# Half-precision value chunks and evenly spread sums in an attention and convolution block

## The chip, the cores and the metric

The kernel runs on one core of one Trainium2 chip. The metric is the time of one execution on the device in microseconds (us).

## What is computed

The reference takes four images of 96 channels and 128 x 128 points, in f32, and adds two branches one after the other:

```
x = x + attention(groupnorm(x))
x = x + convolutions(groupnorm(x))
```

The attention normalizes over the channels, projects to 96 query and 48 key and value channels (24 and 24), and runs a depthwise 3 x 3 convolution over all 144:

```
q  = dwconv3x3(conv1x1(xn, q_w), q_dw)
kv = dwconv3x3(conv1x1(xn, kv_w), kv_dw)
k, v = split(kv)
attn = softmax(l2norm(q) @ l2norm(k).T * temperature)
out  = conv1x1(attn @ v, proj_w)
```

The contraction of `attn` runs over all 16384 points of an image, so it is a small matrix per head. The second branch is a 1 x 1, a 3 x 3, a 5 x 5 and a dilated 3 x 3 convolution, joined by a 1 x 1. Both group norms need sums over a whole image.

## The kernel before, in words

One program goes through the four images (`for b in range(B)`). In each, all engines follow the same order of stages: normalizing and projecting (L844 on PE), the depthwise convolution, the gram product of queries and keys (L902), softmax and attention (L937), and the joined convolutions in units of rows (L1012, L1017). Semaphores written out by hand set the order; each engine has its own list, and what stands behind a wait on an engine waits too. Names in capitals are constants of the program.

**The depthwise stage.** The 144 channels are cut into `DK` = 24 chunks of six: chunks 0 to 19 are queries and keys, 20 to 23 are values. In the planes of a chunk the points' rows lie on the partitions, so that a vertical tap is a product with a band matrix. For each chunk

- DVE builds the band matrices by masking the taps `V` (`bands`, L1493), into one of two buffers: the bands of chunk n start when chunk n-2 is through;
- PE multiplies (`depthwise`): an f32 chunk has three matmuls a channel (L869, which the trace shows as two records each), a chunk in the list `SPLIT` has nine f16 matmuls a channel (L874), on the high and the low half of planes and taps. Results go to three pairs of PSUM banks in turn;
- ScalarE copies the result out (`evict`): L1132 for queries and keys, which are kept as a high half, and L1129 for values, which go back to `Q` in f32;
- DVE forms the low half of queries and keys (`low_parts`, L1521).

GpSimd (POOL) cuts the planes of the chunks in `SPLIT` into halves beforehand, three steps a chunk (`split_chunks`, L692 to L694). Image 0 has no split chunk: there POOL prepares the weights of the convolutions instead. Once, in image 0 behind the strips, DVE cuts the taps into halves (`packed_taps`, L1506 to L1512), one run of chunks after the other. Chunks 6 to 17 of an image are a hardware loop on PE, the others are straight code.

**The sums of the next image.** Group norm needs the sums and the sums of squares of the next image before it starts. SP brings that image in 32 pieces (`AT`) of four rows through three buffers (`stage_rows`), a piece's load when the piece three before it is summed. Between its evictions ScalarE sums each piece twice with an accumulating activation (`next_sums`: L1140 plain, L1146 squared). Behind an even chunk stands one piece, behind an odd chunk two, until there are none left.

**Behind the stage.** DVE waits for all 32 pieces (`s_ns`), copies the first strip of queries and keys (`strip`, L1540), and adds up the sums (`moments`, L1395 to L1398). PE waits for the same sums and for the third step of the moments, makes the group mean's product (`group_mean`, L818), and goes on to the eight gram products (`gram`, L902):

```
pe.wait_ge(s_ns, (b + 1) * AT + START)
pe.wait_ge(s_qd, (b + 1) * DK - 1 + START)
group_mean(st, MEANX, sv + N_MEANN, 3)
```

**Setup.** Before image 0 DVE takes the statistics of that image (L1340) and the scales of the taps (L1361 to L1376, L1438 to L1440).

Of the kernel before, what the change touches and what calls it, by code (L numbers as in the profile page):

```python
# [25 lines left out]
def build_program(nc, x, ln_w, ln_b, q_w, q_dw, kv_w, kv_dw, proj_w, temperature, w1, w3, w5, wd, wf, out):  # L26
    f32, f16, bf16, i32 = mybir.dt.float32, mybir.dt.float16, mybir.dt.bfloat16, mybir.dt.int32
    ALU = mybir.AluOpType
    ACT = mybir.ActivationFunctionType
    AX = mybir.AxisListType  # L30

    B, C, H, W = x.shape
    P = 128
# [3 lines left out]
    KC = KV // 2  # L37
    HD = C // HEADS
    CO = C + KV
    QK = C + KC  # L40
# [4 lines left out]
    AT = H // AR  # L45
# [50 lines left out]
    with ctx:  # L96
# [38 lines left out]
        V = sb("V", [P, 3, 3 * CO])  # L135
# [10 lines left out]
        ps = ctx.enter_context(nc.psum_tensor("ps", [P, 8, BANK], f32))  # L146
# [21 lines left out]
        T = work[:, 1536:1536 + 2 * DM * BW].rearrange("p (i m x) -> p i m x", i=2, m=DM)  # L168


        SPLIT = (2, 4, 5, 7, 8, 10, 11, 13, 14, 16, 17, 19)
        SPLIT_RUNS = (slice(2, 18, 3), slice(4, 20, 3))
        NS = len(SPLIT)
        MASK = 6
        LOW, HIGH = 0, 1
# [66 lines left out]
        rawdw = Qf[:, 7392:7392 + 9 * CO].rearrange("p (m d) -> p m d", d=3)  # L242
# [15 lines left out]
        tapsum = Qf[:, 10200:10200 + QK]  # L258

        def col(i, n=C):  # L260
            return small[0:n, i:i + 1]
# [3 lines left out]
        OSC_MHALF, OSC_MSIXTH, OSC_SIXTH, OSC_THIRD, OSC_THIRDS, OSC_HALF = range(37, 43)  # L265
        QKS, CLAMP, WMAX, TMAX, BMAX = 43, 44, 45, 46, 47
        QSC, QINV = 26, 30
        MEANX, VARX, SAX, SBIX, MG2 = 23, 24, 27, 28, 29
        OSCS = ((OSC, 1.0), (OSC_MHALF, -0.5), (OSC_MSIXTH, -1.0 / 6), (OSC_SIXTH, 1.0 / 6), (OSC_THIRD, 1.0 / 3),
                (OSC_THIRDS, 2.0 / 3), (OSC_HALF, 0.5))  # L270
# [34 lines left out]
        s_vscaled = plain_sem("depthwise_taps_scaled")  # L305
# [5 lines left out]
        s_qd = sem("stored_chunk")  # L311
# [45 lines left out]
        s_wt = plain_sem("weights_placed")  # L357

        NLOADS = 13
        N_BOUND, N_RES, N_QKS, N_AMAX, N_WSC = 6, 9, 23, 28, 31  # L360
        N_QKV = N_WSC + len(OSCS) + 3
        N_COPIES = 4
        N_TURNED = 3 * (3 + 2)
        N_SPLIT = 13 + NRT * 6 + 2
# [182 lines left out]
        def _(pool):  # L547
# [115 lines left out]
            for b in range(B):  # L663
# [15 lines left out]
                def split_chunks():  # L679

                    pool.wait_ge(s_pq, (b + 1) * AT + START)
                    pool.wait_ge(s_out, b * UNITS * 16 + START)
                    pool.wait_ge(s_packed, 3 * len(SPLIT_RUNS))
                    steps = Steps(s_qs, (b - 1) * 3 * NS + START)

                    def step(ins):
                        steps.done(ins)
                        pool.wait_ge(s_qs, steps.value())
                    for m in SPLIT:
                        words = Q[:, m * DC:(m + 1) * DC, :].rearrange("p c h -> p (c h)")  # L690
# [76 lines left out]
        def _(pe):  # L767
# [63 lines left out]
            for b in range(B):  # L831
# [46 lines left out]
                for n in range(6):  # L878
                    depthwise(n, n, SPLIT.index(n) if n in SPLIT and b else None)
                with pe.Fori(0, 2) as k6:  # L880
                    for at in range(6):
                        depthwise(k6 * 6 + 6 + at, at, k6 * 4 + SPLIT.index(6 + at) if at % 3 and b else None)
                for n in range(18, DK):
                    depthwise(n, n, SPLIT.index(n) if n in SPLIT and b else None)

# [144 lines left out]
        def _(act):  # L1030
# [47 lines left out]
            for b in range(B):  # L1078
# [36 lines left out]
                if b < 1:  # L1115
                    act.wait_ge(s_V, N_TURNED)
                    act.wait_ge(s_dv, N_QKV)
                    act.activation(V[:, :, 0:3 * QK], V[:, :, 0:3 * QK], ACT.Copy, scale=col(QKS, P)).then_inc(s_vscaled, 1)
                    act.activation(V[:, :, 3 * QK:], V[:, :, 3 * QK:], ACT.Copy, scale=col(QINV, P)).then_inc(s_vscaled, 1)
                    act.wait_ge(s_dv, N_WSC)  # L1120
                    for k in range(5):
                        act.activation(folded[:, k], folded[:, k], ACT.Copy, scale=col(WSC)).then_inc(s_fold, 1)

                def evict(n):
                    k2, i = divmod(n, 2)
                    bank = 2 * (n % 3)
                    act.wait_ge(s_dw, b * DK + n + 1 + START)
                    if n >= 2 * GROUPS_QK:
                        act.activation(Q[:, n * DC:(n + 1) * DC, :].rearrange("p (k c) h -> p k (c h)", k=2),  # L1129
                                       ps[:, bank:bank + 2, 0:3 * H], ACT.Copy).then_inc(s_qd, 1)  # L1130
                        return
                    act.activation(HL[:, k2, :, DC * i:DC * (i + 1)].rearrange("p h (k c) -> p h k c", k=2),  # L1132
                                   ps[:, bank:bank + 2, 0:3 * H].rearrange("p k (c h) -> p h k c", c=3),
                                   ACT.Copy).then_inc(s_qd, 1)

                def next_sums(c, j, loads, first=False):

                    act.wait_ge(s_nl[j], loads * 16 + START)
                    act.wait_ge(s_ns, b * AT + c + START)
                    act.activation(stage[j], stage[j], ACT.Copy,  # L1140
                                   accum_out=nsums[:, bass.ds(c, 1)]).then_inc(s_nt, 1)
                    act.wait_ge(s_nt, b * AT + c + 1 + START)
                    if first:
                        act.activation(col(NSH), nsums[:, 0:1], ACT.Copy, scale=-1.0 / BANK).then_inc(s_nsh, 1)
                        act.wait_ge(s_nsh, b + 1 + START)
                    act.activation(stage[j], stage[j], ACT.Square, bias=col(NSH),  # L1146
                                   accum_out=nsums[:, bass.ds(AT + c, 1)]).then_inc(s_ns, 1)

                for n in range(DK):
                    k2, i = divmod(n, 2)  # L1150
                    evict(n)
                    for j in ((0,) if i == 0 else (1, 2)):
                        c = k2 * 3 + j
                        if c < AT:
                            next_sums(c, j, b * (11 if j < 2 else 10) + k2 + 1, c == 0)
                act.wait_ge(s_qd, (b + 1) * DK + START)

                def values(k):
# [168 lines left out]
        def _(dve):  # L1327
            v = nc.vector
            setup = Steps(s_dv)

            def link(steps, ins):
                steps.done(ins)
                dve.wait_ge(steps.s, steps.value())
# [18 lines left out]
            for k in range(3):  # L1352
# [9 lines left out]
                                        apply_absolute_value=True))  # L1362
# [11 lines left out]
            link(setup, v.tensor_scalar(col(BMAX, P).bitcast(i32), col(BMAX, P).bitcast(i32), 0x7F800000, None, ALU.bitwise_and))  # L1374
            link(setup, v.reciprocal(col(QKS, P), col(BMAX, P)))
            link(setup, v.tensor_scalar(col(QKS, P), col(QKS, P), 16384.0, None, ALU.mult))  # L1376
            assert setup.n == N_QKS
            statistics(6, len(TAKEN))

# [58 lines left out]
            link(setup, v.tensor_tensor(col(CLAMP, P), col(QKS, P), col(QKS, P), ALU.mult))  # L1438
            link(setup, v.tensor_scalar(col(CLAMP, P), col(CLAMP, P), 1e-24, None, ALU.mult))
            link(setup, v.tensor_tensor(col(QKS, P), col(QKS, P), col(QINV, P), ALU.mult))  # L1440
            assert setup.n == N_QKV

            for b in range(B):
# [36 lines left out]
                def bands(n, parts):  # L1480
# [5 lines left out]
                    dve.wait_ge(s_vscaled, 2)  # L1486
                    if b and n in SPLIT:
                        dve.wait_ge(s_packed, 3 * len(SPLIT_RUNS))
# [108 lines left out]
                with dve.Fori(0, SETS // 2) as k2:  # L1597
                    for k in range(2):
                        for j in range(2):
                            n = (b * (SETS // 2) + k2) * 4 + k * 2 + j  # L1600
# [263 lines left out]
                for r in range(OR):  # L1864
                    n = len(range(r, LASTR, OR))
# [30 lines left out]
```

## Time and profile before

| | |
|---|---|
| Time, median of 3 runs | 1664.78 us (1664.50 to 1666.73) |
| The profiled execution | 1664.77 us, of which the span from the first to the last instruction is 1663.0 us |
| Busy on PE, DVE, ScalarE, POOL | 97%, 88%, 63%, 39% of the span |
| Mean granted clock of TensorE | 0.975 of full speed |

The span is that of the profile's first to last instruction; the rest of the execution's time lies around it. A matmul's end is modelled, so a busy PE is not a PE at its peak. Times in the rows are microseconds from the span's start. The depthwise stages begin near 102, 510, 911 and 1312 us.

### The profile page before, as it was taken

The page shows a single profiled execution, that of the slowest core. Times are in us where ns is not written, and L with a number is a line of the kernel's source. Part 1 is how long each engine was busy: PE and PEld are TensorE (multiplying, and loading weights), DVE is VectorE, ACT ScalarE, POOL GpSimd, SP SyncE. Part 2 cuts the span into 40 slices and gives each one's busy share as a digit, 9 for nine tenths or more (in the row PEclk, how much of TensorE's full clock was granted, in tenths as well). Part 3 has the DMA queues.
Part 4 walks back from the last instruction along what each step waited for, and adds up shares of the span by engine and source line. Part 5 has one row for each costly group of instructions (what it writes and reads, how often), then busy time and mean ns, then how long its engine had stood idle before and what let it go on. Part 6 is the DMA issues. An engine that isn't in the chain of part 4 may idle for free.

```text
span 1663.0 us, 38439 instructions
## 1 busy us (share of the span) xinstructions
PE 1605.5 (97%) x13933; PEld 1524.3 (92%) x13933; DVE 1456.9 (88%) x1949; ACT 1040.2 (63%) x1667; POOL 655.7 (39%) x507
## 2 busy tenths in 40 slices
PE   6999989999999999999999999899999999899998
PEld 5999959999999986999999996899999999599998
DVE  6788789999789959999978986999988897799996
ACT  4877676555286868645546776765446677765651
POOL 4888031222289303232248903023226950312232
PEclk9999979999999997999999998899999999799999
DMA  7012205666502202666630220366661131054553
GB/s 197 0 42 73 71 5 138 171 164 180 151 18 59 81 16 48 158 169 178 171 101 15 73 67 1 89 175 176 170 167 48 34 85 36 16 137 127 145 149 100
DMA packets 105042, 166.37 MB, mean 100 GB/s; under 512 B 40266, under 2 KB 78763, under 8 KB 104780
## 3 DMA queue, kind: packets, MB, share of 16 engines
q1 hardware_dynamic: 81772, 138.95, 33.1%
q10 hardware_dynamic: 23168, 26.04, 5.1%
q8 instruction: 65, 1.06, 0.3%
q14 instruction: 37, 0.30, 0.1%
HBM read 52.20 MB, written 25.17 MB: 47 GB/s over the span
## 4 chain that ended last, share of the span: by engine, by line
PE 80%; DVE 9%; issue 6%; ACT 3%; SPq 1%; DMA 1%; DVEq 0%; ACTq 0%
PE ps L1017 41%; PE ps L869 14%; PE ps L844 12%; PE ps L874 7%; PE ps L902 3%; DVE region L1765 1%; PE ps L1012 1%; DVE region L1493 1%; ACT region L1237 1%; DVE region L1340 1%; ACT region L1168 1%; DVE region L1790 1%; ACT region L1193 1%; DVE region L1762 1%; ACT region L1218 0%
## 5 line engine op out<-in xcount | busy, mean ns | idle before, releaser
L1017 PE MATMUL ps<-region,W 128*96 128x256 f16 (+2 forms) x7140 | 790.6, 271 | 16.0 <-DVE region L1790 8.0
L1017 PEld LDWEIGHTS ps<-region,W 128*96 128x96 f16 (+1 forms) x7140 | 779.1, 122 | 19.8 <-DVE region L1790 9.5
L1493 DVE TENSOR_TENSOR region<-V,ps 128x2322 int32<-128x2322 int32 (+2 forms) x104 | 246.9, 2384 | 37.0 <-issue 30.9
L1237 ACT ACTIVATE region<-region 96x1584 f16<-96x1584 f32 (+2 forms) x80 | 98.4, 1272 | 287.5 <-DVE region L1699 287.5
L748 POOL TENSOR_TENSOR region<-region 96x528 f32<-96x528 f32 (+1 forms) x72 | 96.4, 1343 | 437.9 <-DVE region L1765 238.5
L869 PE MATMUL ps<-region 128*128 (+2 forms) x2160 | 248.7, 276 | 8.6 <-DVE region L1493 4.7
L869 PEld LDWEIGHTS ps<-region 128*128 128x128 f32 x2160 | 243.7, 192 | 12.4 <-issue 7.5
L844 PE MATMUL ps<-proj,region 96*128 96x240 f32 x1024 | 208.5, 367 | 0.0
L844 PEld LDWEIGHTS ps<-proj,region 96*128 96x128 f32 x1024 | 194.6, 190 | 12.8
L667 POOL TENSOR_TENSOR region<-region,cbias 128x576 f32 (+1 forms) x124 | 175.7, 1417 | 57.9 <-DVE region L1465 54.2
L738 POOL TENSOR_TENSOR region<-region,X 96x1536 f32<-96x1536 f32 x40 | 116.0, 2901 | 190.1 <-DVE region L1820 190.1
L1765 DVE TENSOR_TENSOR region<-region 96x1056 f16<-96x1056 f32 (+6 forms) x160 | 175.7, 1154 | 0.6 <-ACT region L1242 0.5
L1790 DVE SCALAR_TENSOR_TENSOR region<-ps,small,region 96x768 f32<-96x768 f32 (+1 forms) x176 | 163.9, 989 | 13.2 <-PE ps L1017 11.5
L714 POOL TENSOR_TENSOR region<-X 96x512 f32<-96x512 f32 (+1 forms) x16 | 29.1, 1841 | 268.5 <-PE ps L937 268.5
L874 PE MATMUL ps<-region 128*128 (+2 forms) x1944 | 120.2, 220 | 0.1
L874 PEld LDWEIGHTS ps<-region 128*128 128x128 f16 x1944 | 116.2, 98 | 2.6 <-issue 0.2
L1132 ACT ACTIVATE region<-ps 128x768 f16<-128x768 f32 x80 | 65.6, 820 | 81.1 <-PE ps L869 69.5
L1231 ACT ACTIVATE region<-region 96x1584 f16<-96x1584 f16 (+3 forms) x88 | 113.9, 1295 | 0.4
L1820 DVE TENSOR_TENSOR region<-region 96x256 f32<-96x256 f32 (+3 forms) x176 | 89.0, 546 | 24.2 <-DMA out_dram<-region 22.6
L1465 DVE TENSOR_TENSOR region<-ps,region 128x576 f32<-128x576 f32 x124 | 94.0, 758 | 12.3
L1086 ACT ACTIVATE region<-X,small 96x512 f32 (+1 forms) x128 | 101.6, 803 | 0.3 <-DVE small L1391 0.3
L1092 ACT ACTIVATE region<-ps 128x384 f32<-128x384 f32 x128 | 62.7, 490 | 54.0 <-PE ps L844 50.9
(249 smaller groups left out, 2139.8 us busy)
## 6 DMA issues: line engine op xcount, KB each, us to landing
region<-region SPq DMA_DIRECT2D x104, 247.5 KB, 4.2
region<-in_x_dram SPq DMA_DIRECT2D x128, 192.0 KB, 2.4
out_dram<-region SPq DMA_DIRECT2D x40, 576.0 KB, 4.3
region<-region ACTq DMA_DIRECT2D x72, 247.5 KB, 2.5
X<-in_x_dram SPq DMA_DIRECT2D x30, 576.0 KB, 6.2
region<-region SPq DMA_DIRECT2D x32, 247.4 KB, 5.1
X<-in_x_dram SPq DMA_DIRECT2D x19, 384.0 KB, 10.4
region<-region SPq DMA_DIRECT2D x24, 185.6 KB, 3.9
```

The lines of the kernel that those rows point to most:

```text
L667: pool.tensor_tensor(Q[:, :, bass.ds(t * AR, AR)].rearrange("p c r -> p r c"), pq[:, i], cbias[:].unsqueeze(1).broadcast_to([P, AR, CO]), ...
L738: pool.tensor_tensor(ob[:, 0:r * W], ob[:, 0:r * W], X[:, bass.ds(u * UR * W, r * W)], ALU.add).then_inc(s_res, 1)
L844: last = mm(ps[:, 2 * i + r // 2, r % 2 * 256:r % 2 * 256 + NP], y1[:, i, r * W:(r + 1) * W], proj[:], start=True, stop=True)
L869: last = mm(o[:, to], T[:, i, 3 * c + d, 0:W], src[:, of], start=k == 0, stop=k == 2)
L874: last = mm(o[:, to], T16[:, i, 3 * c + d, 0:W, te], parts[qe][:, of], start=k == t == 0, stop=k == t == 2)
L1017: last = mm(o, w, src, start=opens and k == 0, stop=k == len(steps) - 1, skip_group_check=g in (2, 4) or split and ck > 0)
L1086: act.activation(y1[:, i, :], X[:, bass.ds(t * BANK, BANK)], ACT.Identity, bias=col(SBIX), scale=col(SAX)).then_inc(s_y1, 1)
L1231: act.activation(hi2[0:C, a:e, x:z], hi[0:C, a:e, x:z], ACT.Copy).then_inc(s_h, 1)
L1237: act.activation(dst[0:C, a:e, x:z], src, ACT.Copy, scale=1.0 if whole else col(SA)).then_inc(s_h, 1)
L1493: v.tensor_tensor(T[:, i, 3 * c:3 * c + m].bitcast(i32).rearrange("p m (i j) -> p m i j", j=3), taps.broadcast_to([P, m, BW // 3, 3]), mas ...
L1765: v.tensor_tensor(low[:, :, x:end], src, hi[0:C, a:e, x:end], ALU.subtract).then_inc(s_l, 1)
L1790: step = lambda dst, g, factor, src: v.scalar_tensor_tensor(row(dst), product(i, g, blocks), col(factor), row(src), ALU.mult, ALU.add).the ...
```

## The change

Value chunks 20 to 23 are put on the list `SPLIT`, with a third run of taps. In images 1 to 3 POOL cuts their planes too and PE takes them in f16 halves. Values get a scale of their own: DVE reduces their taps in the setup (two reductions) and makes a power of two (five column steps); the taps of the values are multiplied by `VKS`, and the eviction multiplies by `VUN`, a column, to undo it.

ScalarE's sums are dealt out anew: behind chunk n stand the pieces from n + ceil(n/3) to n + floor(n/3) + 1, that is two behind chunks 0, 3, 6 and so on, and one behind each of the others. The last piece, number 31, now stands behind chunk 23; it stood behind chunk 21.

```
-        SPLIT = (2, 4, 5, 7, 8, 10, 11, 13, 14, 16, 17, 19)
-        SPLIT_RUNS = (slice(2, 18, 3), slice(4, 20, 3))
+        SPLIT = (2, 4, 5, 7, 8, 10, 11, 13, 14, 16, 17, 19, 20, 21, 22, 23)
+        SPLIT_RUNS = (slice(2, 18, 3), slice(4, 20, 3), slice(20, 24))
...
-                    act.activation(V[:, :, 3 * QK:], V[:, :, 3 * QK:], ACT.Copy, scale=col(QINV, P)).then_inc(s_vscaled, 1)
+                    act.activation(V[:, :, 3 * QK:], V[:, :, 3 * QK:], ACT.Copy, scale=col(VKS, P)).then_inc(s_vscaled, 1)
...
-                                       ps[:, bank:bank + 2, 0:3 * H], ACT.Copy).then_inc(s_qd, 1)
+                                       ps[:, bank:bank + 2, 0:3 * H], ACT.Copy, scale=col(VUN, P)).then_inc(s_qd, 1)
...
                 for n in range(DK):
-                    k2, i = divmod(n, 2)
                     evict(n)
-                    for j in ((0,) if i == 0 else (1, 2)):
-                        c = k2 * 3 + j
-                        if c < AT:
-                            next_sums(c, j, b * (11 if j < 2 else 10) + k2 + 1, c == 0)
+                    for c in range(n + -(-n // 3), n + 1 + n // 3 + 1):
+                        next_sums(c, c % 3, b * (11 if c % 3 < 2 else 10) + c // 3 + 1, c == 0)
...
+            link(setup, v.tensor_reduce(tapsum[:, 0:KC], rawdw[:, 3 * QK:3 * CO, :].rearrange("p (c m) d -> p c (m d)", m=3), AX.X,
+                                        ALU.add, apply_absolute_value=True))
+            link(setup, v.tensor_reduce(col(VTMAX, P), tapsum[:, 0:KC], AX.X, ALU.max))
             assert setup.n == N_QKS
             statistics(6, len(TAKEN))
...
+            link(setup, v.tensor_scalar(col(VTMAX, P), col(VTMAX, P), 1e-20, None, ALU.max))
+            link(setup, v.tensor_scalar(col(VTMAX, P).bitcast(i32), col(VTMAX, P).bitcast(i32), 0x7F800000, None, ALU.bitwise_and))
+            link(setup, v.reciprocal(col(VKS, P), col(VTMAX, P)))
+            link(setup, v.tensor_scalar(col(VKS, P), col(VKS, P), 2.0 ** 7, None, ALU.mult))
+            link(setup, v.tensor_scalar(col(VUN, P), col(VTMAX, P), col(QINV, P), 2.0 ** -7, ALU.mult, ALU.mult))
             assert setup.n == N_QKV
```

On ScalarE, at the end of the depthwise stage of image 0, from the eviction of chunk 21 to the copies of the values. Before (L1129 is the eviction, L1140 and L1146 are one piece, L1161 the first copy of the values; the waits are given by semaphore, `depthwise_chunk` being PE's chunk):

```order
L1129 ACTIVATE region<-ps 128x768 [waits depthwise_chunk]
L1140 ACTIVATE region,nsums<-region 96x512 [waits next_rows_summed,next_rows_staged1]
L1146 ACTIVATE region,nsums<-region,small 96x512 [waits next_rows_totalled]
L1129 ACTIVATE region<-ps 128x768 [waits depthwise_chunk] x2
L1161 ACTIVATE region<-region 128x4x4x24 [waits stored_chunk]
```

and in the changed kernel, where the same lines are L1130, L1141, L1147 and L1159:

```order
L1130 ACTIVATE region<-ps,small 128x768 [waits depthwise_chunk]
L1141 ACTIVATE region,nsums<-region 96x512 [waits next_rows_summed,next_rows_staged1]
L1147 ACTIVATE region,nsums<-region,small 96x512 [waits next_rows_totalled]
L1141 ACTIVATE region,nsums<-region 96x512 [waits next_rows_summed,next_rows_staged2]
L1147 ACTIVATE region,nsums<-region,small 96x512 [waits next_rows_totalled]
L1130 ACTIVATE region<-ps,small 128x768 [waits depthwise_chunk]
L1141 ACTIVATE region,nsums<-region 96x512 [waits next_rows_summed,next_rows_staged0]
L1147 ACTIVATE region,nsums<-region,small 96x512 [waits next_rows_totalled]
L1130 ACTIVATE region<-ps,small 128x768 [waits depthwise_chunk]
L1141 ACTIVATE region,nsums<-region 96x512 [waits next_rows_summed,next_rows_staged1]
L1147 ACTIVATE region,nsums<-region,small 96x512 [waits next_rows_totalled]
L1159 ACTIVATE region<-region 128x4x4x24 [waits stored_chunk]
```

Chunk 21 has two pieces behind it, chunk 22 one, and the last piece of the image stands behind the eviction of chunk 23, where the copies of the values followed at once.

On PE, the end of the stage of image 1: the last channel of chunk 23, the group mean's product and the start of the gram. Before:

```order
L869 MATMUL ps<-region 128x128
L869 MATMUL ps<-region 128x127 x2
L818 MATMUL ps<-small,gmean 96x1 [waits image_vector_steps,stored_chunk,next_rows_summed]
L902 MATMUL ps<-region 120x240 [waits query_key_strips,query_key_low_parts]
L902 MATMUL ps<-region 120x240 x15
```

and in the changed kernel:

```order
L875 MATMUL ps<-region 128x128 x3
L875 MATMUL ps<-region 128x127 x6
L819 MATMUL ps<-small,gmean 96x1 [waits image_vector_steps,stored_chunk,next_rows_summed]
L903 MATMUL ps<-region 120x240 [waits query_key_strips,query_key_low_parts]
L903 MATMUL ps<-region 120x240 x15
```

Each channel of the chunk has nine matmuls in place of three; the product behind it waits for the sums (`next_rows_summed`) and for DVE's moments (`image_vector_steps`) as it did.

## Rows read from the trace of the kernel before

**Rows 1.** The page's chain that ended last, shares of the span by engine.

```profile
PE 80%; DVE 9%; issue 6%; ACT 3%; SPq 1%; DMA 1%; DVEq 0%; ACTq 0%
```

**Rows 2.** Timeline of PE, image 1: start, us, engine, line, operation, tiles, count.

```profile
526.47 6.46 PE L874 MATMUL ps<-region 128*128 128x128 f16 x108
...
536.96 6.98 PE L874 MATMUL ps<-region 128*128 x108
544.11 4.28 PE L869 MATMUL ps<-region 128*128 x36 [0.17 <-DVE region L1521]
...
584.74 16.29 PE L869 MATMUL ps<-region 128*128 128x128 f32 x144
600.87 0.25 PE L818 MATMUL ps<-small,gmean 96*96 96x1 f32 x2
600.99 6.75 PE L902 MATMUL ps<-region 128*120 128x240 f16 x64
```

**Rows 3.** Timeline of ScalarE (ACT), image 1; in brackets the idle time before.

```profile
544.15 0.79 ACT L1132 ACTIVATE region<-ps 128x768 f16<-128x768 f32 x1
...
593.03 0.81 ACT L1129 ACTIVATE region<-ps 128x768 f32<-128x768 f32 x1 [1.76 <-PE ps L869]
593.74 0.62 ACT L1140 ACTIVATE region<-region 96x512 f32<-96x512 f32 x1
...
595.11 0.19 ACT L1146 ACTIVATION_READ_ACCUMULATOR region<-region,small 96x1 f32 x1
...
601.07 0.81 ACT L1129 ACTIVATE region<-ps 128x768 f32<-128x768 f32 x1 [3.21 <-PE ps L869]
```

**Rows 4.** Timeline of DVE, the end of the stage in image 1.

```profile
587.70 0.95 DVE L1521 TENSOR_TENSOR region<-ps,region 128x768 f16<-128x768 f32 x1
...
593.09 2.57 DVE L1493 TENSOR_TENSOR region<-V,ps 128x2322 int32<-128x2322 int32 x1 [1.45 <-PE ps L869]
595.58 0.65 DVE L1540 COPY region<-region 128x1920 f16<-128x1920 f16 x1
...
596.60 0.15 DVE L1398 TENSOR_SCALAR small<-small 96x1 f32<-96x1 f32 x1
```

**Rows 5.** Timeline of POOL, image 1: first and last split, and what follows.

```profile
509.59 0.82 POOL L692 CAST region<-region 128x768 f16<-128x768 f32 x1
...
553.47 1.06 POOL L694 COPY region<-region 128x768 f16<-128x768 f16 x1
624.87 2.98 POOL L714 TENSOR_TENSOR region<-X 96x512 f32<-96x512 f32 x2 [70.34 <-PE ps L937]
```

**Rows 6.** Timeline of PE, image 0: the first grams.

```profile
199.45 6.75 PE L902 MATMUL ps<-region 128*120 128x240 f16 x64
```

**Rows 7.** Timeline of DVE: the setup, and image 0 around the packing of taps.

```profile
24.34 1.25 DVE L1361 TENSOR_REDUCE region<-region 128x120 f32<-128x1080 f32 x1
...
48.13 0.55 DVE L1450 TENSOR_REDUCE region<-region 128x4 f32<-128x384 f32 x1 [1.74 <-ACT region L1092]
...
208.97 0.47 DVE L1506 CAST region<-V 128x108 f16<-128x108 f32 x3
...
214.22 0.28 DVE L1571 SCALAR_TENSOR_TENSOR region<-region,ps 120x120 f32<-120x120 f32 x1 [1.85 <-ACT region L1177]
```

**Rows 8.** Timeline of PE: the convolutions' first matmuls in images 0, 1 and 3.

```profile
250.43 4.48 PE L1017 MATMUL ps<-region,W 128*96 128x256 f16 x24 [2.28 <-DMA region<-region]
...
652.34 2.83 PE L1017 MATMUL ps<-region,W 128*96 128x256 f16 x24 [1.88 <-DMA region<-region]
...
1472.47 6.60 PE L1017 MATMUL ps<-region,W 128*96 128x256 f16 x43 [2.46 <-DVE region L1790]
```

**Rows 9.** Busy time by stretch: stretch, us, five engines, granted clock (PEclk), DMA, GB/s.

```profile
251.00:254.00 3.00, 3.00 (x16) 2.85 (x15) 3.00 (x2) 3.00 (x3) 0.00 (x0) 0.50 0.33 67
...
653.50:656.50 3.00, 3.00 (x29) 2.80 (x27) 2.97 (x3) 3.00 (x3) 0.00 (x0) 1.00 0.14 27
...
1473.00:1476.00 3.00, 3.00 (x16) 2.85 (x15) 2.96 (x4) 0.00 (x0) 0.00 (x0) 0.50 0.78 182
```

More of the change, by code:

```diff
@@ L267, in build_program @@
         QSC, QINV = 26, 30
+        VTMAX, VKS, VUN = BMAX, WMAX, QSC
         MEANX, VARX, SAX, SBIX, MG2 = 23, 24, 27, 28, 29
@@ L359, in build_program @@
         NLOADS = 13
-        N_BOUND, N_RES, N_QKS, N_AMAX, N_WSC = 6, 9, 23, 28, 31
-        N_QKV = N_WSC + len(OSCS) + 3
+        N_BOUND, N_RES, N_QKS, N_AMAX, N_WSC = 6, 9, 25, 30, 33
+        N_QKV = N_WSC + len(OSCS) + 8
         N_COPIES = 4
```

## The prediction

> **What bounds the kernel now.** I read the chain of waits first: 80% of the span runs over PE and 9% over DVE [rows 1]. Of the lines that the chain names only L869 and L874, the depthwise matmuls, and L902, the gram matmuls behind them, are near the change, so I went to the timeline of that stage, engine by engine, in image 1 (images 2 and 3 repeat it).
>
> PE runs two half-precision chunks, 108 matmuls, in 6.46 us, or 3.2 us each; the four value chunks, in f32, fill 16.29 us without a gap, 4.02 us from one eviction to the next (593.03 to 601.07 for two). Right behind them, at 600.87, comes the group mean's product and at 600.99 the first gram matmul [rows 2, 3]. So here PE is the limit, and the others wait for it.
>
> On ScalarE the reader should see when the last piece is summed: it stands behind chunk 21 (593.03), runs from 593.74 to the accumulator read of 595.11, and is done at 595.30, almost six microseconds before PE needs it [rows 3]. DVE takes its first strip and the moments at 595.58, right behind its last band, and the third moment is done at 596.75 [rows 4]. The product at 600.87 waits for that moment, which now costs nothing because chunks 22 and 23 cover it. **This cover is what the change moves.**
>
> **Part 1, the value chunks in half precision (images 1 to 3).** Four chunks go from 4.02 to 3.2 us. Counted from 584.74, chunk 23 would end near 597.5 and its eviction start near 597.7, against 601.07 (the eviction starts 0.2 us behind the last matmul's successor, 600.87 to 601.07) [rows 2, 3]. DVE makes one band a chunk, 2.57 us, which fits into 3.2; at one place it has low parts to do first, 0.95 us at 587.70, so that the band of chunk 22 comes near 591.2 where PE would want it at 591.1 [rows 4]. I add 0.15 us for that: the eviction of chunk 23 at 597.9, **3.2 us earlier per image**.
>
> For such a pair of weight load and matmul with 128 columns, the Trainium skill (TensorE: Matmul & The Clock Gate, Back-to-back issue gap) gives some 81 ns sustained in a real kernel. By that a chunk of 54 would take an estimated 4.4 us, more than the f32 chunk, and the sum below would be 14 us larger. The trace differs: 108 such matmuls in 6.46 us are 60 ns each [rows 2].
>
> POOL splits 16 chunks where it split 12. The twelve took from 509.59 to 554.53, 3.75 us each; four more end near 569.5. Chunk 20 starts at 584.74, and POOL is idle for 70 us behind its last split [rows 2, 5]. Cost: nothing; the cover is 15 us, and gone it would hold chunk 20. The scale at the eviction is an operand in place of a constant: nothing.
>
> **Part 2, the sums spread evenly (all four images).** Pieces 28 and 29 go behind chunk 21, 30 behind 22 and 31 behind 23, the last chunk. Two pieces between two evictions are 3.1 us and an eviction 0.71, more than a half-precision chunk, so one eviction in three still comes late by some 0.6 us; PE is three chunks behind, so this costs nothing. The staging loads are issued as pieces finish, and SP's queue holds the weight placement of image 0 behind the last of them; it moves by two chunks, some 8 us, and its user, the convolution, starts at 250.43, fifty microseconds behind the stage [rows 6, 8]. Nothing.
>
> What costs is the end. From the start of chunk 23's eviction: 0.71 us to the piece (593.03 to 593.74), 1.56 for the piece (593.74 to 595.30), 0.1 to wake DVE, 1.17 for the strip and three moments (595.58 to 596.75), 0.1 to wake PE, 0.12 from the mean's product to the first gram matmul. That makes **3.76 us from that eviction to the first gram matmul**, where it now starts 0.08 us before the eviction [rows 2 to 4]. The wakes are the only parts without a row; between nothing and 0.2 each.
>
> - Image 0 stays f32: gram moves from 199.45 to 199.45 + 0.08 + 3.76 = 203.3, that is **+3.84 us** [rows 6].
> - Images 1 to 3: 597.9 + 3.76 = 601.66 against 600.99, **+0.67 us each, +2.0** in all. The gain of part 1 is eaten by the wait.
>
> Behind that, grams are limited by PE, strips 1 to 3 come off DVE faster than PE uses them, ScalarE's copies of the values start at about the old time, and all follow the gram. So the shift goes through to the end.
>
> **Part 3, setup.** Two more DVE reductions stand in the statistics, where DVE runs without idle up to the first normed tile. A reduction of 1080 elements takes 1.25 us; the new ones have 216 and 24 elements. Between 0.3 and 1.25, I take the nearer end with the issue between: **+0.6 us**. Five column steps come later, in front of an idle of 1.74 us: nothing [rows 7]. In image 0 the packing has a third, smaller run: the two present ones take from 208.97 to 212.37, 1.70 us each, and DVE idles 1.85 us behind them until 214.22 [rows 7]. Nothing.
>
> Sum so far: 0.6 + 3.84 + 2.0 = **+6.4 us**.
>
> **Part 4, the clock.** PE now idles some 3.6 us between chunk 23 and the mean's product, in every image. At the start of the convolution the trace has such idles. After 2.28 us (image 0) and 2.46 us (image 3) the granted clock is at the lower level, 0.50, or 1.2 GHz, in the following microseconds; after 1.88 us (image 1) it stays at 1.00 [rows 8, 9]. The same 24 matmuls take 4.48 us in image 0 and 2.83 in image 1: a fall costs 1.65 us. The new idle is longer than those that were followed by a fall, but part of the low stretch can lie in the idle itself, and the gram's shape has no row at the lower level. Bounds: 0 and 4 x 1.65 = 6.6 us. I take three falls of four, **+5.0 us**, nearer to the upper end because of the two rows.
>
> Total: 6.4 + 5.0 = +11.4. The profiled execution took 1664.77 us, the median of the runs is 1664.78, so they are one: **1676.2 us**, or 0.7% slower.
>
> **The rivals.**
> A. The wait, but no fall of the clock: +6.4, **1671.2 us**. For it: image 1's idle went without one. Against it: the new idle is almost twice as long.
>
> B. Half-precision chunks lose their pace when five stand in a row (19 to 23). In the loop, 536.96 to 544.11 is 7.15 us for two, 3.58 each, against 3.2 in straight code; there address arithmetic stands between the matmuls. If five in a row go at 3.58, the gain shrinks by 0.38 x 4 x 3 = 4.6 us: **1680.8 us** [rows 2]. Against it: chunks 20 to 23 are straight code. The Trainium skill's page named in part 1 (TensorE: Matmul & The Clock Gate) would go further in this direction.
>
> C. Not slower. The loop's pairs lose 7.15 - 6.4 = 0.75 us, and there are four in an image. The eviction at 544.15 begins only then, since two pieces stood before it [rows 2, 3]. If late evictions hold PE there, and the even spread ends that, 0.75 x 4 x 3 = 9.0 us come back: 6.4 - 9.0 = -2.6, **1662.2 us** without a fall of the clock, 1667.2 with three. It decides from 6.4 us up. Against it: chunk 9 needs chunk 6's bank, freed long before; straight-code pairs show no loss though their evictions are late as well; and the new order again puts two pieces before the eviction of a half-precision chunk.
>
> **How the numbers follow.** Forecast 0.62, A 0.17, B 0.12, C 0.09. The range runs from just under A, with shorter wakes and reductions, to B: **1669 to 1681 us**. A measurement of this kernel can tell about 0.2%, 3.3 us, from no change; below 1668.1 counts as the same. The forecast and B lie above, A almost always, C below: slower 0.89, same 0.08, faster 0.03.
>
> **What would show it.** In the changed profile: evictions of chunks 20 to 23 some 3.2 us apart in images 1 to 3, and the last near 3.2 us earlier from the stage's start; a piece behind chunk 23, with DVE's first strip waiting for ScalarE, not for its own band; an idle of PE of about 3.6 us before the mean's product in all four images; granted clock 0.50 in part of the grams of about three. The span from stage start to the first gram grows by 3.8 us in image 0 and 0.7 in the others. I am wrong if PE's idle there is under 2 us, if value chunks take 3.6 us, or if the loop's pairs get shorter.

## The result, and the profile after

The changed kernel takes **1676.24 us** (median of 4 runs, 1675.00 to 1677.84) against 1664.64 for the kernel before (4 runs, 1663.03 to 1666.73). The ratio is 1.007, with a 95% interval of 1.0052 to 1.0087: slower. The profiled execution took 1675.66 us, of which 1673.9 are the span, 10.9 more than the span before.

The page's chain, which answers to [rows 1]:

```profile
PE 78%; DVE 10%; issue 6%; ACT 4%; DMA 1%; SPq 1%; ACTq 1%; DVEq 0%
```

PE's share of the chain is two points lower, DVE's and ScalarE's one higher each. Two points of the span are 33 us, more than the 10.9 it grew by, and in the kernels of the experiments PE's share stands between 75 and 82% without following the time; so the wait is read from the timelines and not from these shares. The timeline of PE in image 1, against [rows 2]:

```profile
542.87 6.96 PE L875 MATMUL ps<-region 128*128 x108
550.01 4.28 PE L870 MATMUL ps<-region 128*128 x36 [0.17 <-DVE region L1527]
...
587.50 16.13 PE L875 MATMUL ps<-region 128*128 128x128 f16 x270
...
607.38 0.30 PE L819 MATMUL ps<-small,gmean 96*96 96x1 f32 x2 [3.75 <-DVE small L1399]
607.54 8.41 PE L903 MATMUL ps<-region 128*120 128x240 f16 x64
```

Five half-precision chunks, 270 matmuls, stand in one block. Behind them PE idles for 3.75 us, which ends on DVE's third moment (L1399). Then the 64 grams take 8.41 us where they took 6.75. ScalarE and DVE at the same place, against [rows 3] and [rows 4]:

```profile
594.00 0.90 ACT L1130 ACTIVATE region<-ps,small 128x768 f32<-128x768 f32 x1 [0.18 <-PE ps L875]
...
603.67 0.90 ACT L1130 ACTIVATE region<-ps,small 128x768 f32<-128x768 f32 x1 [0.24 <-PE ps L875]
604.47 0.61 ACT L1141 ACTIVATE region<-region 96x512 f32<-96x512 f32 x1
...
605.84 0.19 ACT L1147 ACTIVATION_READ_ACCUMULATOR region<-region,small 96x1 f32 x1
```

```profile
606.06 0.66 DVE L1546 COPY region<-region 128x1920 f16<-128x1920 f16 x1 [6.27 <-ACT region L1147]
607.09 0.15 DVE L1399 TENSOR_SCALAR small<-small 96x1 f32<-96x1 f32 x1
```

The links follow one another with no gap above 0.14 us: last eviction 603.67, piece 604.47 to 606.03, strip 606.06, third moment done at 607.24, product 607.38, gram 607.54. DVE had stood idle for 6.27 us, waiting for the piece that now stands behind the last chunk.

The granted clock at the grams of image 0 and image 1 (stretch, us, PE, PEld, DVE, ACT, POOL, PEclk, DMA, GB/s), and below it the same place in the kernel before:

```profile
205.00:208.20 3.20, 3.20 (x18) 3.20 (x17) 3.10 (x15) 2.73 (x4) 0.00 (x0) 0.50 0.45 81
607.90:610.90 3.00, 3.00 (x17) 3.00 (x16) 2.95 (x13) 2.72 (x4) 0.00 (x0) 0.50 0.01 3
```

```profile
601.10:609.10 8.00, 8.00 (x81) 8.00 (x80) 5.24 (x17) 5.79 (x8) 0.00 (x0) 1.00 0.00 0
```

Behind the wait the clock stands at its lower level, 0.50 (1.2 GHz), for about the first three microseconds of the grams. In images 2 and 3 the grams start at 1010.11 and 1413.84 us, PE idles 3.75 us ahead of the product again, and the 64 grams take 8.41 and 8.11 us.

Where the 10.9 us arose, from the starts of the stages in the two timelines (us):

| stretch | image 0 | image 1 | image 2 | image 3 | sum |
|---|---|---|---|---|---|
| up to the depthwise stage of image 0 | +1.26 | | | | +1.26 |
| stage start to first gram | +3.95 | +0.64 | +0.47 | +0.80 | +5.86 |
| the first 64 grams, at the lower clock | +1.66 | +1.66 | +1.66 | +1.36 | +6.34 |
| the rest of the image | -0.96 | -0.35 | +0.86 | -2.11 | -2.56 |

### The profile page after: what moved, and what is told of

It is laid out like the page before. It is cut to its first block, busy times and chain, and to the rows that moved or that the text cites. A ratio compares the mean times of both kernels' runs of the same rounds, so it can differ in the third digit from the quotient of the medians.

```text
span 1673.9 us, 38947 instructions
## 1 busy us (share of the span) xinstructions
PE 1598.3 (95%) x14149; PEld 1517.3 (91%) x14149; DVE 1458.8 (87%) x1965; ACT 1039.7 (62%) x1667; POOL 699.1 (42%) x543
## 4 chain that ended last, share of the span: by engine, by line
PE 78%; DVE 10%; issue 6%; ACT 4%; DMA 1%; SPq 1%; ACTq 1%; DVEq 0%
PE ps L1018 39%; PE ps L845 12%; PE ps L870 11%; PE ps L875 9%; PE ps L903 4%; DVE region L1771 1%; DVE region L1499 1%; PE ps L1013 1%; ACT region L1235 1%; DVE region L1338 1%; DVE region L1796 1%; ACT region L1166 1%; ACT region L1191 1%; DVE region L1768 1%; ACT region L1216 0%
## 5 line engine op out<-in xcount | busy, mean ns | idle before, releaser
L870 PE MATMUL ps<-region 128*128 (+2 forms) x1728 | 199.8, 276 | 8.5 <-DVE region L1499 4.7
L870 PEld LDWEIGHTS ps<-region 128*128 128x128 f32 x1728 | 195.2, 192 | 12.2 <-issue 7.3
L1796 DVE SCALAR_TENSOR_TENSOR region<-ps,small,region 96x768 f32<-96x768 f32 (+1 forms) x176 | 163.9, 989 | 12.6 <-PE ps L1018 10.9
L875 PE MATMUL ps<-region 128*128 (+2 forms) x2592 | 158.5, 220 | 0.1
L875 PEld LDWEIGHTS ps<-region 128*128 128x128 f16 x2592 | 154.1, 98 | 3.2 <-issue 0.7
```

Of the source, the lines that this page charges most:

```text
L870: last = mm(o[:, to], T[:, i, 3 * c + d, 0:W], src[:, of], start=k == 0, stop=k == 2)
L875: last = mm(o[:, to], T16[:, i, 3 * c + d, 0:W, te], parts[qe][:, of], start=k == t == 0, stop=k == t == 2)
L1796: step = lambda dst, g, factor, src: v.scalar_tensor_tensor(row(dst), product(i, g, blocks), col(factor), row(src), ALU.mult, ALU.add).the ...
```

## Experiments

Each kernel was timed in five rounds beside the kernel before on the same chip. The kernel before took 1664.58 us in the first group (9 runs, 1662.28 to 1666.39), 1664.72 in the second (9 runs, 1662.09 to 1665.94) and 1664.56 in the third (15 runs, 1662.55 to 1666.35). Three questions: does the place of the last piece cost what the chain says, what is each part worth alone, and what is the clock's share? One execution of each kernel was profiled. Over the runs of one kernel the mean granted clock goes, for instance, from 0.970 to 0.980 (the change), so the falls of the clock in a trace are those of that execution, and other executions may have others.

### The new order of the sums alone

The kernel before, with the changed kernel's loop on ScalarE and nothing else:

```
                 for n in range(DK):
-                    k2, i = divmod(n, 2)
                     evict(n)
-                    for j in ((0,) if i == 0 else (1, 2)):
...
+                    for c in range(n + -(-n // 3), n + 1 + n // 3 + 1):
+                        next_sums(c, c % 3, b * (11 if c % 3 < 2 else 10) + c // 3 + 1, c == 0)
```

> The kernel before, with the new order of the sums alone; value chunks stay in f32. Theory (the last piece behind chunk 23 puts a wait of 3.8 us and a fall of the clock before the gram): every image pays 3.84 us, 15.4 us in all, and for each fall up to 1.65 us, so 1680 to 1687 us, with PE idle for some 3.7 us before the group mean in all four images. Rival (the sums' order is harmless, and what costs is the split): 1663 to 1667 us, no new idle.

**1687.1 us** (4 runs), ratio 1.0135 [1.0119, 1.015]. PE in image 1:

```profile
611.15 0.30 PE L818 MATMUL ps<-small,gmean 96*96 96x1 f32 x2 [3.66 <-DVE small L1395]
611.32 8.41 PE L902 MATMUL ps<-region 128*120 128x240 f16 x64
```

All four images pay the wait: counted from the stage's start the first gram comes 3.86, 3.91, 3.94 and 3.83 us later, 15.54 together. All four pay the clock too: the 64 grams take another 1.66, 1.66, 2.88 and 1.66 us, 7.86 together. With +1.66 at the start of the first stage this makes 25.1; the profiled execution, the longest of the four at 1689.74 us, has a span of 1688.0 against 1663.0. The rest of the images goes up and down by one or two microseconds and sums to nothing. So the new order of the sums costs 22.5 us by itself (1687.1 - 1664.58).

### The half-precision chunks alone

The changed kernel with the old loop on ScalarE, two pieces behind odd chunks, the last piece behind chunk 21:

```
+                    k2, i = divmod(n, 2)
                     evict(n)
-                    for c in range(n + -(-n // 3), n + 1 + n // 3 + 1):
-                        next_sums(c, c % 3, b * (11 if c % 3 < 2 else 10) + c // 3 + 1, c == 0)
+                    for j in ((0,) if i == 0 else (1, 2)):
+                        c = k2 * 3 + j
+                        if c < AT:
+                            next_sums(c, j, b * (11 if j < 2 else 10) + k2 + 1, c == 0)
```

> The changed kernel with the sums in the old order (the last piece behind chunk 21); value chunks split. Theory: 3.2 us gained in each of three images, 0.7 us lost in the setup, so 1653 to 1658 us, no idle of PE before the gram, four value chunks in some 12.9 us. Rival (with faster chunks the two pieces behind odd chunks hold PE, or the split chunks lose their pace): 1661 us or more, value chunks 3.6 us each.

**1652.58 us** (5 runs, 1652.49 to 1654.79), ratio 0.9936 [0.9922, 0.9949]. This version beats both kernels. PE, and DVE's first strip, in image 1:

```profile
582.00 16.13 PE L875 MATMUL ps<-region 128*128 128x128 f16 x270
597.97 0.28 PE L819 MATMUL ps<-small,gmean 96*96 96x1 f32 x2
598.10 6.75 PE L903 MATMUL ps<-region 128*120 128x240 f16 x64
```

```profile
594.20 0.65 DVE L1549 COPY region<-region 128x1920 f16<-128x1920 f16 x1
```

The strip is done three microseconds before the last chunk ends, PE goes from chunk to gram without idle, and the grams keep the full clock. Stage start to first gram is shorter by 3.27, 3.46 and 3.30 us in images 1 to 3, 10.0 together; two more came off the convolution of image 3 in this trace, where the last two experiments look. So the changed kernel has a gain of some 10 us in it, and its own order of the sums takes 23.7 us away again (1676.24 - 1652.58).

### Evenly spread, but done two chunks earlier

The changed kernel with its 32 pieces spread over chunks 0 to 21:

```
-                    for c in range(n + -(-n // 3), n + 1 + n // 3 + 1):
+                    for c in range(min(AT, -(-n * AT // 22)), min(AT, -(-(n + 1) * AT // 22))):
```

> The changed kernel with the sums spread evenly over chunks 0 to 21: 32 pieces, one or two behind each of them, none behind 22 and 23. Theory (an even spread gains nothing by itself, only its end matters): as with the split alone, 1653 to 1658 us, and chunks 0 to 19 take as long as before. Rival (late evictions hold PE in the loop's pairs of split chunks, and an even spread frees them): the pairs shrink from 7.15 us towards 6.4, up to 9 us less, 1645 to 1650 us.

**1654.76 us** (5 runs), ratio 0.9937 [0.9924, 0.9951], not to be told from the version before this one. The first pair of the loop in image 1:

```profile
538.65 6.98 PE L875 MATMUL ps<-region 128*128 x108
545.80 4.28 PE L870 MATMUL ps<-region 128*128 x36 [0.17 <-DVE region L1527]
```

This pair takes 545.80 - 538.65 = 7.15 us, as before. All twelve pairs of the loop in images 1 to 3 together take 84.6 us, against 84.9 in the kernel before and 84.7 in the change. Within the spread of the runs, even spreading by itself gains nothing and costs nothing; the place of the last piece costs.

### The last piece once more behind chunk 23

Piece 30 is moved from chunk 22 to chunk 23, so that two pieces stand behind the last eviction:

```
-                    for c in range(n + -(-n // 3), n + 1 + n // 3 + 1):
+                    for c in (30, 31) if n == 23 else () if n == 22 else range(n + -(-n // 3), n + 1 + n // 3 + 1):
```

> The changed kernel with piece 30 moved from behind chunk 22 to behind chunk 23, so that two pieces stand behind the last chunk. Theory: the wait before the gram grows by one piece, 1.5 to 1.6 us, in each of four images: PE idles 5.3 us in place of 3.75, and the time grows by 6.2 us to some 1682 us; if the longer idle lets a second low stretch of the clock follow, up to 1689. Rival (the sums are not what PE waits for): as the changed kernel, 1676 us.

**1685.35 us** (4 runs), ratio 1.0126 [1.011, 1.0141].

```profile
612.13 0.45 PE L819 MATMUL ps<-small,gmean 96*96 96x1 f32 x2 [5.41 <-DVE small L1399]
612.44 9.36 PE L903 MATMUL ps<-region 128*120 128x240 f16 x64
```

The idle grows from 3.75 to 5.41 us, 1.66 for one piece, in all four images. The grams take 9.21, 9.36, 8.11 and 9.08 us, 8.8 over four times 6.75 where the change had 6.3. So a piece behind the last eviction stands on the path at its full length.

### TensorE kept busy in the wait

Fourteen matmuls of the identity with itself, whose result nobody reads, ahead of PE's wait for the sums:

```
+                keep_warm(7, 14)
                 pe.wait_ge(s_ns, (b + 1) * AT + START)
```

> The changed kernel with fourteen unused matmuls of 128 columns in f32 on PE in front of the wait for the sums, 3.3 us of work inside the idle of 3.75 us. Theory: the first grams run slowly since the clock falls after the idle; kept busy, the first 64 grams take 6.75 us in place of 8.41 in every image, some 6.4 us less in all if nothing else moves, 1669 to 1673 us. The wait itself stays. Rival (the grams are slow because DVE's strips come late): still 8.4 us, 1676 us or, if the filler delays the mean, more.

**1671.99 us** (5 runs), ratio 1.004 [1.0026, 1.0054].

```profile
602.09 3.34 PE L814 MATMUL ps<-ident 128*128 128x128 f32 x28
606.00 0.30 PE L819 MATMUL ps<-small,gmean 96*96 96x1 f32 x2 [0.57 <-DVE small L1400]
606.16 6.75 PE L903 MATMUL ps<-region 128*120 128x240 f16 x64
```

```profile
606.20:609.20 3.00, 3.00 (x32) 3.00 (x32) 2.93 (x13) 3.00 (x4) 0.00 (x0) 1.00 0.04 8
```

With the idle cut to 0.57 us the clock stays at 1.00 and the 64 grams take 6.75 us in all four images. The wait itself stays: the gram still starts 3.91 us behind the last matmul (606.16 - 602.25, the end of the block). DVE's strips come no earlier than in the change (the first starts 1.49 us before the gram here, 1.48 there), so they are not what slowed the grams. Wait and clock are two costs. The time falls by 4.25 us, where the grams had lost 6.34; the last table of these experiments shows where most of the rest went.

### The mean's product behind the first gram

The gram does not read the group mean; it only stands behind it on PE. Here the product is issued behind the first of the eight gram products:

```
-                group_mean(st, MEANX, sv + N_MEANN, 3)
                 pe.wait_ge(s_qkl, (b + 1) * 2 * GROUPS_QK + START)
                 for k in range(VPAIRS):
                     gram(k)
+                    if k == 0:
+                        group_mean(st, MEANX, sv + N_MEANN, 3)
```

> The changed kernel with the group mean's product behind the first gram in place of ahead of it, so that the first gram waits for DVE's first strip alone and no longer for the three moments. Theory (the chain is piece, strip, moments, mean, in that order): the first gram starts at the end of the strip and not 0.8 us after it, in four images, 2.9 us less or 1673 us, with an idle of 3.1 us still. Rival (PE waits for ScalarE's copies or for something else behind the sums): no change, 1676 us.

**1672.15 us** (5 runs), ratio 1.0048 [1.0034, 1.0062].

```profile
606.96 2.12 PE L903 MATMUL ps<-region 128*120 128x240 f16 x16 [3.23 <-DVE region L1547]
...
1009.23 1.82 PE L903 MATMUL ps<-region 128*120 128x240 f16 x16 [3.23 <-DVE region L1547]
```

The gram now waits for the strip alone, 3.23 us, 0.68 less than the 3.91 of the change, or 2.7 for four images. In image 2 the same 3.23 us of idle was not followed by a fall: the first 16 grams took 1.82 us, against 2.35, 2.12 and 2.69 in the others. There the granted clock is 1.00 from the first gram on, so this trace has one fall less.

### Filler ahead of the convolutions

Most of what the changed kernel gave back lies in the convolutions, where the trace of before has falls of the clock as well [rows 8, 9]. Two kernels have six filler products more ahead of the convolution in every image, one on top of the version with half-precision chunks alone, one on top of the kernel before:

```
                 group_mean(st, VG, sv + N_VG2, 7)
-                keep_warm(0, 22)
+                keep_warm(0, 28)
```

> Half-precision value chunks with the old order of the sums, and six filler products more (28 in place of 22) ahead of the convolution in every image. Without the six, that kernel's trace shows TensorE idle for 2.13 us (image 0) and 2.25 us (image 3) ahead of the first convolution matmul, granted clock 0.50 behind it, and the first 24 matmuls take 4.48 us in image 3 in place of 2.83. Theory (the low clock there follows the idle): the filler takes up 0.7 to 1.4 us of the idle, no start moves, the two falls go, 2 x 1.65 = 3.3 us less, 1649.3 us. Rival (the falls there don't hang on this idle, or move to a later wait): 1652.6 us, no change. Second rival: in an image where the filler runs at the low clock it ends behind the DMA that the convolution waits for, and the start moves by up to 0.3 us an image: 1652.6 to 1654 us.

**1656.85 us** (5 runs), ratio 0.9953 [0.994, 0.9967]: four microseconds slower than without the filler, where 1649.3 was expected.

> The kernel before with the same six filler products more ahead of the convolution in every image. Its trace has falls of the granted clock behind that idle in images 0 (idle 2.28 us) and 2 (2.39 us), and one behind an idle of 2.46 us within the convolution of image 3, which the filler does not touch. Theory (the low clock follows the idle): two falls go, 2 x 1.65 = 3.3 us less, 1661.4 us, and the first convolution matmuls of image 0 take 2.83 us in place of 4.48. Rival (the falls don't hang on this idle, or move): 1664.7 us, no change.

**1664.9 us** (11 runs), ratio 1.0 [0.9991, 1.001]: no change.

In both, the theory put on record failed. The traces have no fall at the start of a convolution any more, but falls at a later wait. Image 1 without the filler (first fence) and with it (second):

```profile
649.10 2.83 PE L1018 MATMUL ps<-region,W 128*96 128x256 f16 x24 [1.25 <-DMA region<-region]
653.07 0.64 PE L1013 MATMUL ps<-region,W 96*96 96x256 f16 x4 [1.15 <-DMA region<-region]
...
668.40 4.97 PE L1018 MATMUL ps<-region,W 128*96 128x256 f16 x43 [1.37 <-DVE region L1799]
```

```profile
640.49 8.60 PE L814 MATMUL ps<-ident 128*128 128x128 f32 x56
649.18 2.83 PE L1018 MATMUL ps<-region,W 128*96 128x256 f16 x24
651.97 0.64 PE L1013 MATMUL ps<-region,W 96*96 96x256 f16 x4
...
668.15 6.61 PE L1018 MATMUL ps<-region,W 128*96 128x256 f16 x43 [2.22 <-DVE region L1799]
```

In both, PE waits a second time some 19 us into the convolution, for a step of DVE (L1799, L1790 before). Behind it the same 43 matmuls take 4.97 us at the full clock and 6.61 with a fall. The second wait ends as far behind the first gram with the filler as without, image by image to 0.03 us in both pairs of kernels; here it is 668.40 - 598.10 = 70.30 without the filler and 668.15 - 597.87 = 70.28 with it. Where the first convolution matmul waited for a DMA, the second wait ends 19.3 us behind that matmul. In image 3 of before, where the convolution starts as follows, that is 1472.47 - 1453.16 = 19.31 [rows 8]:

```profile
1453.16 2.83 PE L1017 MATMUL ps<-region,W 128*96 128x256 f16 x24 [1.25 <-DMA region<-region]
```

So the row of image 3 in [rows 8] is this second wait, and not the start of a convolution, as the heading there and the prediction took it to be.

Since the second wait ends when it does, what PE loses ahead of it, to a wait or to the low clock, comes off this second idle, and what it saves there makes the idle longer. A fall behind it is paid in full. In image 2 of the kernel before, the filler took the fall at the start away and the second idle grew, with a fall behind it; without the filler (first fence) and with it (second):

```profile
1052.77 4.47 PE L1017 MATMUL ps<-region,W 128*96 128x256 f16 x24 [2.39 <-DMA region<-region]
1072.07 4.97 PE L1017 MATMUL ps<-region,W 128*96 128x256 f16 x43 [1.07 <-DVE region L1790]
```

```profile
1052.18 2.83 PE L1017 MATMUL ps<-region,W 128*96 128x256 f16 x24 [0.43 <-ACT region L1237]
1071.16 6.56 PE L1017 MATMUL ps<-region,W 128*96 128x256 f16 x43 [2.25 <-DVE region L1790]
```

This is the rival on record, a fall that moves. The version with half-precision chunks is not as clear: its new falls stand in images 1 and 2, where there was none at the start to save. There the second idle grew because a wait of 1.15 (1.07 in image 2) for a DMA ahead of L1013 is gone; it is gone in images 1 and 3 of the kernel before too, without added filler, and why is not shown. The second rival of this version came true as well: in image 1 the filler ran at a mean granted clock of 0.74, took 8.60 us and ended behind the DMA, so the convolution started 0.31 us later behind the gram. In image 0 of the kernel before it came 0.83 later.

The length of the convolution stage, from its first matmul to the next image's first projection (image 3: to the end of the span), in us, with the place of a fall:

| kernel | image 0 | image 1 | image 2 | image 3 |
|---|---|---|---|---|
| before | 203.56 start | 202.25 none | 202.32 start | 209.88 second wait |
| the change | 202.62 none | 202.25 none | 203.18 none | 207.77 none |
| kept busy | 202.27 start | 203.84 second wait | 203.90 second wait | 207.76 none |
| chunks alone | 202.76 start | 202.25 none | 202.24 none | 207.77 start |
| chunks and filler | 202.45 none | 203.72 second wait | 203.89 second wait | 207.76 none |
| before and filler | 201.49 none | 202.25 none | 203.52 second wait | 209.41 second wait |

In images 2 and 3 a fall at the start costs nothing (202.32 and 202.24; 207.77 and 207.77): the second wait covers it. In image 0 other waits differ too, and the table does not tell. A fall at the second wait costs 1.3 to 2.1 us. This is also where the kernel with TensorE kept busy lost part of its gain again, in images 1 and 2.

## Why the prediction came out

The time, 1676.24 us, is the forecast's 1676.2. A hit as close as that is luck: the terms are not as exact.

**The value chunks.** Forecast was an eviction of chunk 23 that comes 3.2 us earlier. From the start of chunk 20 to that eviction it is 603.67 - 587.50 less the 3.14 of chunk 19 that opens the block, or 13.03 us (chunk 19 is 581.60 to 584.74 in the kernel before), against 16.33 in [rows 2, 3]: 3.30 earlier. The evictions of chunks 20 and 23 start 9.67 us apart, 3.22 a chunk. POOL's splits stayed hidden. The last ends at 575.57, forecast was 569.5, which with the stage's shift of 5.91 is 575.4; POOL is then idle until attention:

```profile
574.51 1.06 POOL L695 COPY region<-region 128x768 f16<-128x768 f16 x1
632.73 2.98 POOL L715 TENSOR_TENSOR region<-X 96x512 f32<-96x512 f32 x2 [57.16 <-PE ps L938]
```

One entry of this part was wrong: "The scale at the eviction is an operand in place of a constant: nothing." The eviction takes 0.90 us where it took 0.81, and the piece follows it by 0.80 in place of 0.71 [rows 3]. On the path that is 0.09 us an image: PE's idle is 3.75 us in the change and 3.66 with the new order alone, whose eviction has the constant.

**The wait.** Forecast 3.76 us from the last eviction to the first gram, measured 3.87 (603.67 to 607.54); the 0.09 above is most of the difference. The two wakes, which stood at 0.1 us each without a row, came out at 0.03 (606.03 to 606.06) and 0.14 (607.24 to 607.38). Image 0 was to lose 3.84 and lost 3.95, images 1 to 3 were to lose 2.0 together and lost 1.91. The order alone (waits in all four images) and the piece moved once more (+1.66 each) bear the chain out. ScalarE's idles at the end of the stage in image 1 all end on PE, none on the load of a piece.

**Setup.** The two new reductions take DVE from 30.26 to 30.88, 0.62 us; forecast 0.6.

```profile
30.26 0.38 DVE L1375 TENSOR_REDUCE region<-region 128x24 f32<-128x216 f32 x1
30.67 0.18 DVE L1377 TENSOR_REDUCE small<-region 128x1 f32<-128x24 f32 x1
30.88 8.40 DVE L1338 BATCH_NORM_STATS2 region<-X 96x6 f32<-96x512 f32 x14
...
221.10 0.28 DVE L1577 SCALAR_TENSOR_TENSOR region<-region,ps 120x120 f32<-120x120 f32 x1 [0.40 <-ACT region L1175]
```

The stage started 1.26 us later all the same. Kernels without the setup's change did so by 0.44 (before with filler) and 1.66 us (order alone), so no more than the reductions' share can be put down to the change. The third packing run fits: 0.40 us of idle is left behind it where 1.85 stood.

**The clock: the step that failed in its parts.** The prediction took "three falls of four" at 1.65 us each, +5.0. All four images fell, and the grams lost 6.34; the price per fall was right here (1.66 three times, 1.36 once). It is not a fixed price: with the new order alone one fall took 2.88 us, with two pieces behind the last chunk four took 1.36 to 2.61. The term also counted new falls only. The kernel before has falls of its own, and one of them went: in image 3 the wait within the convolution is as long as before, 2.42 us in place of 2.46 [rows 8], but behind it 43 matmuls take 4.97 us where they took 6.60. That is 1.63 of the 2.11 us that came back in image 3; what gave the rest is not shown. Images 0 and 2 differ by other waits (two of DVE's of 0.9 us together less in image 0, one for a DMA of 0.73 more in image 2). The rest is -0.35 ahead of image 1's attention. So the clock and the stages behind the grams gave +3.8 in place of +5.0, and with +7.1 in place of +6.4 for the other terms the sum came out within the spread of the runs. The prediction was right in sign and mechanism; its exactness is errors that cancel. It had also read the trace of before too narrowly: between the idles of 1.88 and 2.46 us that it compared stands one of 2.44 in image 1, with no fall behind it.

```profile
671.64 4.97 PE L1017 MATMUL ps<-region,W 128*96 128x256 f16 x43 [2.44 <-DVE region L1790]
```

**The rivals.** A (no fall) is wrong: all grams run slow behind the idle, and none does with the idle filled. B (slower pace in a long block) is wrong: 270 matmuls in 16.13 us are 60 ns each. The Trainium skill (TensorE: Matmul & The Clock Gate, Back-to-back issue gap) gives some 81 ns for such a pair; the trace disagrees, here as in [rows 2]. C (late evictions hold PE in the loop) is wrong: the pair that it was read from takes 7.14 us in the change (542.87 to 550.01), 7.15 before, and 7.15 with the sums spread and finished early, and all twelve together differ by 0.3 us. Its price of 9.0 us was too high besides: the twelve pairs before take 84.9 us, 8.1 more than twelve of 6.4. The idle behind the first two of an image's four pairs ends on DVE's low parts, not on an eviction.

## What to carry to other kernels

When side work on a helping engine feeds the next stage, look at its last item, not at how evenly it is dealt out: an item moved behind the last chunk puts itself and everything that hangs on it onto the path, at full length. Here every pass paid it. Faster chunks ahead of such a wait keep their worth, since the wait's chain hangs on the last of them: the half-precision chunks took off 12.0 us with the old order of the sums (1664.58 to 1652.58) and 10.9 with the new one (1687.1 to 1676.24). But a change that carries both parts shows only the sum, 0.7% slower here, and hides the part that gains 0.6%. And an idle of TensorE can have two prices, its length and the low clock behind it; the second is paid only where no later wait absorbs it, so a filler is to be tried against the whole span, not judged by the stretch behind it.

## What the runs showed of the hardware that was not expected

- Idles of nearly the same length were followed by either level of the granted clock: 2.46 us with a fall (image 3 of before), 2.44 and 2.42 without (image 1 of before, image 3 of the change); 1.85 with a fall (image 2 with TensorE kept busy, at the second wait); 3.23 us with a fall in three images and without in the fourth. What decides between them was not settled here.
- The filler ahead of the convolutions left no fall at the place that it covered, and the version with half-precision chunks became 4 us slower with it, the kernel before no faster: the clock fell behind the next wait, whose end had not moved.
- A summed piece takes the same 1.56 us behind chunk 21 (before) and behind chunk 23 (the change), while the eviction of values with a column as its scale takes 0.90 us against 0.81 with a constant.
